# First attention of a twelve-layer decoder: an order of units for each engine

## What is computed

```python
q = jnp.tanh(x @ W_charge.T + b_charge)[..., 0]
phi_c = mags * q[..., None] ** jnp.arange(ORDER + 1)
shell = x @ W_shell.T + b_shell
shell = shell / jnp.maximum(jnp.linalg.norm(shell, axis=-1, keepdims=True), 1e-12)
proj = shell @ omega.T + rff_bias
phi_s = jnp.concatenate([jnp.cos(proj), jnp.sin(proj)], axis=-1) * rff_scale
tp = (phi_c[..., :, None] * phi_s[..., None, :]).reshape(b, n, -1)
phi = tp @ W_combine.T
T = jnp.exp(-DIST_COUPLING * jnp.abs(idx[:, None] - idx[None, :]).astype(x.dtype) / DIST_SCALE)
temp = jax.nn.softplus(log_temp) + 0.1
logits = jnp.einsum('bnd,bmd->bnm', phi, phi) * T / temp
attn = jax.nn.softmax(jnp.where(causal, logits, -jnp.inf), axis=-1)
out = jnp.einsum('bnm,bmd->bnd', attn, x @ W_v.T + b_v)
return out @ W_out.T + b_out
...
x = _layernorm(x + _L0_attn_ref(x, ...), axis=-1)
```

## Time and profile before

| | |
|---|---|
| median of three runs | 2170.95 us (2170.48 to 2173.26) |
| profiled execution | 2172.46 us, of it 2170.7 us span of the core |
| TensorE busy | 1771.8 us, 82% of the span, 11797 matmuls |
| VectorE busy | 1427.0 us, 66% |
| ScalarE busy | 1050.1 us, 48% |
| GpSimd busy | 390.4 us, 18% |
| stage l0a | from 15.6 us to about 158.5 us of the span |

### The profile page before, as it was taken

One profiled execution on the slowest core, in us unless ns is written; L12 is line 12 of the kernel. 1 busy time (PEld: TensorE's weight loads), 2 busy tenths in 40 slices (PEclk: granted clock), 3 DMA queues, 4 the chain that ended last, 5 costly groups with the idle time before them and its releaser, 6 DMA issues. The chain is left out here.

```text
span 2170.7 us, 33139 instructions
## 1 busy us (share of the span) xinstructions
PE 1771.8 (82%) x11797; PEld 1029.4 (47%) x11797; DVE 1427.0 (66%) x3243; ACT 1050.1 (48%) x2222; POOL 390.4 (18%) x574
## 2 busy tenths in 40 slices
PE   5769958999966999995778999994479999798682
PEld 3446642333344666663554444442244544465572
DVE  3436667888855655555546677675779999666434
ACT  3336635776723333331535655551367777465220
POOL 0010030000031544443120000001210000100373
PEclk8889978999977999997789999997689999899696
DMA  3000000000015788783000000000000000000474
GB/s 86 0 1 1 2 1 1 1 1 1 1 77 210 277 299 304 304 300 117 1 1 1 1 1 1 1 1 18 0 1 2 1 2 1 1 2 7 127 212 113
DMA packets 42700, 134.37 MB, mean 62 GB/s; under 512 B 7106, under 2 KB 22518, under 8 KB 37355
## 3 DMA queue, kind: packets, MB, share of 16 engines
q1 hardware_dynamic: 32363, 119.08, 15.6%
q0 software_dynamic: 4992, 10.23, 1.6%
q10 hardware_dynamic: 5184, 2.95, 0.5%
HBM read 123.14 MB, written 11.45 MB: 62 GB/s over the span
## 5 line engine op out<-in xcount | busy, mean ns | idle before, releaser
L160 POOL TENSOR_SCALAR rstd<-MV 128x2 f32<-128x2 f32 (+1 forms) x100 | 25.2, 252 | 1070.0 <-DVE MV L128 1064.2
L855 DVE TENSOR_REDUCE l1aM<-PS 128x2 f32<-128x1024 f32 x128 | 152.9, 1220 | 23.7 <-PE PS L611 21.7
L773 ACT ACTIVATE l1aE<-PS 128x512 f32<-128x512 f32 x256 | 140.8, 595 | 48.2 <-PE PS L640 46.7
L1840 PE MATMUL PS<-WB,H 128*128 128x512 f32 x312 | 143.5, 604 | 1.2 <-ACT H L1958 1.2
L773 ACT ACTIVATE l3aE<-PS 128x512 f32<-128x512 f32 (+3 forms) x256 | 102.5, 442 | 46.7 <-PE PS L644 43.8
L2652 ACT COPY PT<-PS 128x512 f32<-128x512 f32 x128 | 69.2, 589 | 94.7 <-PE PS L2563 94.5
L855 DVE TENSOR_REDUCE l3aM<-PS 128x2 f32<-128x256 f32 (+3 forms) x128 | 101.2, 818 | 19.4 <-PE PS L613 18.4
L2742 DVE TENSOR_REDUCE M<-PS 128x1 f32<-128x589 f32 x128 | 92.5, 764 | 26.5 <-PE PS L2552 26.0
L2658 ACT ACTIVATE E<-PS,M 128x589 f32<-128x589 f32 x128 | 95.9, 764 | 16.9 <-DVE M L2742 16.8
L1958 ACT ACTIVATE H<-PS,WB 128x128 f32<-128x128 f32 x156 | 44.6, 368 | 120.8 <-PE PS L1831 117.7
L883 DVE SCALAR_TENSOR_TENSOR l3aE<-l3aE,l3aLB 128x2048 f32<-128x2048 f32 (+1 forms) x64 | 94.9, 1482 | 2.6 <-ACT l3aE L773 2.6
(11 more groups left out here) (671 smaller groups left out, 4457.8 us busy)
## 6 DMA issues: line engine op xcount, KB each, us to landing
WB<-in_experts SPq DMA_DIRECT2D x39, 1798.0 KB
TB<-mixed_tails SPq DMA_DIRECT2D x39, 384.0 KB
WB<-in_experts SPq DMA_DIRECT2D x39, 384.0 KB, 3.6
WB<-in_fold SPq DMA_DIRECT2D x1, 1676.0 KB, 6.9
cols_l2x_sb<-in_cols_l2x SPq DMA_DIRECT2D x1, 1154.0 KB, 9.8
mixed_tails<-in_tails SPq DMA_DIRECT2D x1, 1152.0 KB, 9.4
mixed_rows<-R SPq DMA_DIRECT2D x4, 256.0 KB, 3.0
WB<-mixed_out SPq DMA_DIRECT2D x4, 256.0 KB, 5.7
```

Source lines behind the costliest of these rows:

```text
L773: nc.scalar.activation(E[0:kn, home(m, kt) + j, q0:S], PS[0:kn, 4 + n % 2, q0:S], ACT.Exp, scale=SCALE).then_inc(exp_done, 1)
L855: v.tensor_reduce(M[:, m % 2, qt, 2 * hp:2 * hp + 2], PS[:, bank:bank + 2, 0:kc], AX, ALU.max, negate=True).then_inc(pair_free, 1)
L1840: mm(o, H1[:, i % 3, c * P:(c + 1) * P], mid_w(i, c), start=(c == 0), stop=False)
```

## The change

The single list is replaced by a list for each engine. In the diff the digit behind a letter is the offset to n.

```diff
-    def front(b):
-        return [("P", b), ("T", b), ("J", b), ("X", b), ("F", b)] if b < BT else [None] * 5
-
-    def merged(b):
-        f = front(b + 1)
-        return [("A", b), f[0], ("M", b), f[1], ("S", b), f[2], ("V", b), ("C", b), f[3], ("W", b), f[4], ("Y", b), ("N", b)]
-
-    order = front(0) + [u for b in range(BT) for u in merged(b) if u]
+    def units(first, step):
+        def at(text, n):
+            return [(u[0], n + int(u[1:])) for u in text.split() if n + int(u[1:]) < BT]
+
+        return at(first, 0) + [u for n in range(BT) for u in at(step, n)]
+
+    pe_order = units("P0 T0 J0 X0 F0", "P1 A0 T1 M0 J1 S0 V0 X1 C0 W0 F1 N0")
+    act_order = units("P0 T0 J0 X0 F0", "P1 T1 S0 J1 C0 X1 N0")
+    dve_order = units("P0 T0 J0 X0 F0", "P1 A0 T1 M0 J1 X1 V0 W0 F1 Y0")
+    pool_order = units("P0 T0 J0 X0 F0", "P1 Y0")
...
-        V0 = k.sb("V0", [P, 2, NT, P + 1])
+        V0 = k.sb("V0", [P, 3, NT, P + 1])
...
                     if b:
-                        pe.wait_ge(ctx_done, b)
-                        pe.wait_ge(c_taken, b)
-                        pe.wait_ge(k.statted, 2 * b)
-                        pe.wait_ge(xt_made, b)
+                        held = ((ctx_done, b), (c_taken, b), (k.statted, 2 * b), (xt_made, b))
                     for qt in range(NT):
                         kc = (qt + 1) * P
+                        if b:
+                            pe.wait_ge(*held[qt])
...
-                    if b >= 2:
-                        act.wait_ge(pv_ready, b - 1)
-                    nc.scalar.copy(tiles(V0[:, b % 2, :, 0:P]), PROJ[:, :, :, 0:P]).then_inc(v_taken, 1)
+                    if b >= 3:
+                        act.wait_ge(pv_ready, b - 2)
+                    nc.scalar.copy(tiles(V0[:, b % 3, :, 0:P]), PROJ[:, :, :, 0:P]).then_inc(v_taken, 1)
```

More of the change, by code:

```diff
@@ L1231, in _ @@
             pe.wait_ge(w["landed"], 16)
-            for kind, b in order:
+            for kind, b in pe_order:
                 xt = k.xt(b)
@@ L1295, in _ @@
                         for kt in range(qt + 1):
-                            ins = mm(o, E[:, kt, qt * P:(qt + 1) * P], V0[:, b % 2, kt, :], start=(kt == 0), stop=(kt == qt))
+                            ins = mm(o, E[:, kt, qt * P:(qt + 1) * P], V0[:, b % 3, kt, :], start=(kt == 0), stop=(kt == qt))
                     ins.then_inc(pv_ready, 1)
@@ L1317, in _ @@
             g = nc.gpsimd
-            for kind, b in order:
+            for kind, b in pool_order:
                 if kind == "P":
@@ L1332, in _ @@
             nc.scalar.activation(tc[:, 2:3], tc[:, 1:2], ACT.Ln, bias=k.ones[:, 0:1]).then_inc(ln_t, 1)
-            for kind, b in order:
+            for kind, b in act_order:
                 if kind == "P":
@@ L1394, in _ @@
             step(v.memset(phiK[64:65, :], 1.0))
-            for kind, b in order:
+            for kind, b in dve_order:
                 if kind == "P":
```

## The result

| | before | changed |
|---|---|---|
| median | 2172.11 us (2170.48 to 2176.20, 4 runs) | 2151.08 us (2147.79 to 2151.89, 4 runs) |
| profiled execution | 2172.46 us, span 2170.7 us | 2151.07 us, span 2149.3 us |
| stage l0a, first matmul to the next stage's first | 15.65 to 158.59: 142.94 us | 15.04 to 138.36: 123.32 us |
| TensorE busy in the stage | 95.94 us | 85.07 us |

A forecast was written before the change was run, and what follows sets the result against it. No engine being full, a chain through all of them was taken to bound the steps; order 8.5 us plus clock 2.0 us gave 10.5 us less, from 2170.95 to 2160.5 us, range 2156 to 2167.

The forecast's parts named there:

- The order's terms: Gains and losses along the step's chain from the new unit orders and waits, summed to 8.5 us at the old clock.
- Part 1: P ahead of A: A covers the path from P to T, gaining 1.7 us a step in three steps.
- part 2: J ahead of S, outer product ahead of division: X starts earlier, gaining 1.85 us a step; the table load waits last.
- part 3: X ahead of C: C and the copy of ctx now stand ahead of W and F, losing 1.35 us a step.
- part 5: Third buffer for the values: the copy had no wait for a buffer already, so nothing gained.
- Part 4: Waits ahead of A: the 0.77 us idle goes at three places, 1.9 us together; the split matters only in step 3.
- The rival with twice the price for a table switch: Switching to the Sin costs a second load's length, 3.8 us less gain: 4.7 us gained, 2166.3 us; chance 0.06.
- The clock's term: Denser TensorE work keeps some low-clock phases away: bounds 0 and 4.1 us, the middle taken, 2.0 us.
- full clock: All low phases but that of N go: 12.6 us gained, at most 13.0, 2158.0 us; chance 0.20.
- Slower: Clock stays at 0.72, the level of batch 0's front: 10.5 us lost against 8.5 gained, 2173 us; chance 0.06.
- taken back: Later stages take the time back, so nothing that ends last moves: 2171 us; chance 0.05.
- Low phases moved: Low phases move onto longer products on the chain such as X and F: gain near 2 us, 2169 us; chance 0.08.

The follow-up runs named there:

- before_filled: The kernel before in its own order, with twelve extra bf16 matmuls ahead of T, C and N in each step; ratio 0.9935, stage 131.73 us.
- unsplit: The changed kernel with the four waits ahead of A in one place again; ratio 0.9911, stage 126.90 us.
- early_row: The changed kernel with VectorE's clearing of row 64 of phiQ ahead of its wait for phi; ratio 0.9875, stage 119.35 us.
- p_first: The kernel before with one edit, P of the next batch ahead of A on TensorE and VectorE; ratio 0.9968, stage 137.06 us.
- the last kernel: The changed kernel with C ahead of X, division ahead of outer product, early clearing of phiQ's row 64 and extra matmuls; ratio 0.9856, median 2143.95 us.
- x_first: The kernel before with one edit, outer product ahead of the division and X ahead of C; ratio 1.0015, stage 147.06 us.
- two_buffers: The changed kernel with two buffers for the values instead of three; ratio 0.9898, stage 123.78 us.

## Why the prediction was wrong

The direction was right, and the size was half of what was measured. The sum of the prediction had two terms: the order, 8.5 us, and the clock, 2.0 of at most 4.1.

**The order's terms held.** The old order at a granted clock of 1.00 (step 1 of before_filled) and the changed one at 1.00 (its step 1) give the order by itself:

| link | old order, full clock | changed | difference | predicted |
|---|---|---|---|---|
| phiK to T | 10.35 | 7.50 | -2.85 | -1.7 and -0.4 to -0.77 |
| T to X | 10.37 | 8.68 | -1.69 | -1.85 |
| X to F | 2.74 | 4.11 | +1.37 | +1.35 |
| F to phiK | 4.14 | 4.14 | 0 | 0 |
| step | 27.60 | 24.43 | -3.17 | -2.6 to -3.0 |

The first row holds parts 1 and 4, the last idle time ahead of A included. Part 1 (T earlier), part 2 (the table load as the new last wait), part 3 (C and ctx between X and F) and part 5 (the buffer) came out within 0.4 us. Part 4 did too: the split matters once, in step 3, as unsplit shows. One row was misread there without effect: 42.77 us is the start of a maximum on VectorE; P began at 42.58 and took 1.9 us. The rival with twice the price for a table switch fell: in the changed kernel the Sin starts 0.01 us after its load. The Trainium skill, page "ScalarE: Activation LUTs", section "What ACT_TABLE_LOAD costs", adds a drain of about 1380 ns to each switch; here, where the load is on the chain, no such time shows.

**The clock's term failed.** What the runs give, for the four steps: the kernel before took 119.39 us. The old order with filling would take 25.54 + 27.60 + 27.60 (step 2 put equal to step 1) + 26.53 = 107.3. The changed order took 99.50, and 97.7 with filling. So the filling took at least 12.1 us of low phases from the old order and 1.8 from the changed one; the difference, 10.3, is the clock's share, and 107.3 - 97.7 = 9.6 that of the order: 19.9 together, which is 119.39 - 99.50. Neither filling removed all low phases. With step 0 of the changed order as in early_row (23.01 + 0.35 at a clock of 1.00) and 17.05 x (1 - 0.87) = 2.2 us taken off the old step 3, the shares are about 11 and 9 us, an estimate. The prediction had 2.0 for the clock and 8.5 for the order.

The step that failed is in the paragraph on the clock, in two sentences. First, "N and the start of A are at the lower level behind the 2.33 us idle, and that place stays". The idle time stays (2.33 us in steps 0 to 2 of the changed kernel), the low phase doesn't always: in step 1 the granted clock was 1.00 throughout, from 62 to 76 us, and N, P and A ran full. That alone is 2.35 us at A (5.01 against 2.66), and a filled old order shows the same (phiK to T 10.35 instead of 12.89). In step 2 the low phase came, on P and half of A. Second, the list of low phases had W twice and S once, and left out X: 2.34 us was taken as X's length. It had the evidence beside it. C, four transposes, took 1.12 us in the row just ahead, and I called that the lower clock; twelve transposes in 2.50 us directly behind it couldn't be all at the full clock. At the full clock X takes 1.53. That error stood in the order's term too, where it happened to cancel, since X is in both sides of X to F.

Taken link by link, the kernel before against step 1 of before_filled, the low phases of steps 0 to 2 cost 12 us: phiK to T 2.5 in step 1 and 1.6 in step 2; T to X 1.7 in step 2, which is S as predicted; X to F 1.0, 2.4 and 2.5 in steps 0 to 2, where the list had 1.2 twice for W and nothing for X; F to phiK 0.35.

**The choice of the middle** between 0 and 4.1 was no estimate. The rows gave the price of each low phase, and the idle times of a step went from 8.5 us (2.53 + 2.61 + 0.28 + 2.33 + 0.77) to 5.5 (1.11 ahead of T, 1.39, 0.67 and 2.33 in the rows above); the granted clock of 0.79 and 0.80 in steps 1 and 2 said outright that some 40% of those steps was at half speed. With TensorE busy for 24.06 and 24.70 us in them, a full clock would take off some 10 us (busy time times one minus the clock), where the filled old order lost 9.4 in them with the clock of one still at 0.94., with 0.82 and 0.80, give 9 us. That number was at hand, and it should have been the upper bound instead of the three phases I had listed.

The rivals: full clock, 13.0 us, was the nearest and had the right mechanism with the wrong bound. Slower and taken back did not happen. Low phases moved happened once, onto P in step 0 (phiK to T 8.02 us, against 6.41 in early_row at the full clock), where the old order had run full; it cost 1.6 us there and not the gain.

## What to carry to other kernels

Here several engines take turns on a chain and TensorE waited over 2 us three times in a step, and the reordering paid twice: once for the waits that it hides, and again for the clock that TensorE kept. The second part can be looked for in other kernels with such waits. Take the bound of the second from the granted clock of the stretch and TensorE's busy time in it, not from a list of slow units; and measure a unit's length in a stretch where the clock is 1.00 before it goes into a sum. To see which of the two a change gives, fill the idle times of the old order with matmuls into a free bank: it takes ten lines, it tells the parts apart, and here it was worth 0.65% by itself. Then look where the clock's low phase went: in p_first it left A and fell on P.

## What was not expected of the hardware

- Bf16 matmuls, 1.2 us for twelve, in idle times of 2.3 to 2.6 us took the granted clock of step 1 from 0.79 to 1.00 (36 were used in the old order, 26 in the last kernel).
- The gains of single edits did not add: 4.1 us as a sum, 19.6 together. Each single edit left at least two idle times above 2 us in a step, the whole change one; that this is the reason fits these four runs and isn't proven; unsplit had one such idle time a step, like the changed kernel, and its low phases fell elsewhere. A swap that costs next to nothing in one order (X ahead of C and the outer product ahead of the division, 0.25 us a step) cost 4.1 us of the stage in another.
- The same code behind the stage took 2001.5 to 2017.2 us in fourteen profiled executions. That is 0.7% of the kernel, so a smaller difference between single executions says little; the stage's own stretches say more.
- Why a low phase stayed away from A in step 1 of the changed kernel and came back for P and half of A in step 2 (clock 0.93), with the same 2.33 us idle ahead of N, was not settled: both had the same order and the same waits.
- The granted clock of the front reads 1.00 in the profiles of p_first, x_first and two_buffers, where its twelve transposes took 2.82 us as in the changed kernel's front at 0.71. The lengths of the units are the surer witness; in the four steps both agree.
